# A hybrid scan, attention and FP4 kernel: the scan's input term moves from PSUM to SBUF, six pooled banks for five, two products in 128 rows, a new order of steps

## The reference, cut to what matters

```python
x = x + scan(_layernorm(x), w_in, w_x, w_dt, b_dt, A_log, Dp)
x = x + fp4_ffn(_layernorm(x), w_gate, w_up, w_down)     # F = 704
x = x + linear_attention(_layernorm(x), W_attn, ...)     # 16 heads of 16
x = x + fp4_ffn(_layernorm(x), w_gate, w_up, w_down)

# inside scan; s is the state (16), d the feature (256)
dt  = softplus(dt_low @ w_dt + b_dt) * DT_SPAN + DT_MIN
dA  = dt[:, :, None] * A
inp_term = einsum('bdn,bn,bd->bn', dA, bt, ut)
h   = exp(dA) * h + inp_term[:, None, :]
y   = einsum('bdn,bn->bd', h, ct) + Dp * ut
```

## Time and profile before

| | us |
|---|---|
| median of 3 runs | 2318.24 (2313.72 to 2318.61) |
| the profiled execution | 2323.44 |
| its span, first to last instruction | 2321.7 |
| PE busy | 2053.9 (88%) |
| DVE busy | 2015.2 (87%) |
| ACT busy | 1857.6 (80%) |
| POOL busy | 1271.2 (55%) |

### The profile page before, as it was taken

One profiled execution on the slowest core, in us unless ns is written; L12 is line 12 of the kernel. 1 busy time (PEld: TensorE's weight loads), 2 busy tenths in 40 slices (PEclk: granted clock), 3 DMA queues, 4 the chain that ended last, 5 costly groups with the idle time before them and its releaser, 6 DMA issues. The chain is left out here.

```text
span 2321.7 us, 40659 instructions
## 1 busy us (share of the span) xinstructions
PE 2053.9 (88%) x12844; PEld 1291.1 (56%) x12844; DVE 2015.2 (87%) x3843; ACT 1857.6 (80%) x3544; POOL 1271.2 (55%) x1837
## 2 busy tenths in 40 slices
PE   2558899998989989898999989899998989989997
PEld 0225556474655646465564646556464655647574
DVE  6898988979989898998989899898989889897845
ACT  4788888897978889797888979788797978867463
POOL 6224455655645565564556556465555546554754
PEclk8669999999999999999999999999999999999999
DMA  3452322323132131423213132322323232321000
GB/s 86 121 133 60 105 57 69 85 61 95 53 94 66 50 102 46 111 54 86 74 50 95 54 99 56 93 67 59 87 62 94 58 96 58 90 63 48 6 6 12
DMA packets 104450, 165.97 MB, mean 71 GB/s; under 512 B 15458, under 2 KB 34094, under 8 KB 104238
## 3 DMA queue, kind: packets, MB, share of 16 engines
q1 hardware_dynamic: 104238, 163.37, 26.2%
HBM read 146.55 MB, written 16.78 MB: 70 GB/s over the span
## 5 line engine op out<-in xcount | busy, mean ns | idle before, releaser
L1588 DVE TENSOR_TENSOR_SCAN scan_bufs<-scan_bufs,inp_bank 128x512 f32<-128x512 f32 x512 | 614.4, 1200 | 6.0 <-ACT scan_bufs L987 4.4
L1304 PE MATMUL bank<-w_gu,f_xqT 128*128 128x512 f32 x1024 | 489.1, 623 | 31.6 <-ACT f_xqT L1050 29.3
L981 ACT ACTIVATE scan_bufs<-scan_bufs,a_rows 128x512 f32<-128x512 f32 x512 | 368.9, 724 | 34.5 <-DMA scan_bufs<-dt_copy 34.2
L1319 PE MATMUL bank<-w_dn,f_hqT 128*128 128x256 f32 x1536 | 360.2, 385 | 11.2 <-ACT f_hqT L1050 9.2
L1598 DVE TENSOR_TENSOR scan_bufs<-scan_bufs,c_bank 128x512 f32<-128x512 f32 x512 | 344.0, 672 | 0.3
L1304 PEld LDWEIGHTS bank<-w_gu,f_xqT 128*128 128x128 f32 x1024 | 197.2, 199 | 255.6 <-issue 246.8
L1319 PEld LDWEIGHTS bank<-w_dn,f_hqT 128*128 128x128 f32 x1536 | 286.6, 191 | 80.1 <-issue 33.0
L898 POOL TENSOR_SCALAR_AFFINE_SELECT masked_scores<-masked_scores 128x512 f32<-128x512 f32 x256 | 172.4, 699 | 242.8 <-ACT masked_scores L1050 241.5
L876 POOL TENSOR_TENSOR f_h<-f_h,f_h_scale 128x704 f32<-128x704 f32 x128 | 185.7, 1451 | 180.5 <-DVE f_h L1468 180.5
L987 ACT ACTIVATE scan_bufs<-scan_bufs 128x1024 f32<-128x1024 f32 x256 | 271.6, 1061 | 1.0
L887 POOL TENSOR_TENSOR f_h<-f_h,f_h_lean 128x704 f32<-128x704 f32 x128 | 222.3, 1737 | 85.6 <-DVE f_h L1649 72.6
(11 more groups left out here) (198 smaller groups left out, 4393.9 us busy)
## 6 DMA issues: line engine op xcount, KB each, us to landing
scan_bufs<-dt_copy SPq DMA_DIRECT2D x512, 256.0 KB, 4.1
...
```

Source lines behind the costliest of these rows:

```text
L981: nc.scalar.activation(half, half, ACT.Exp, scale=a_rows[:, c, at:at + 1]).then_inc(root_ready, 1)
L1304: last = nc.tensor.matmul(to[:, :], f.xqT[:, k, :], w_gu[:, k, g, lo:hi], start=(k == 0), stop=(k == DH - 1))
L1319: last = nc.tensor.matmul(to[:, 0:D], f.hqT[:, k, :], w_dn[:, k, :], start=(k == 0), stop=(k == FK - 1))
L1588: nc.vector.tensor_tensor_scan(half, half, inp[:, :], 0.0, ALU.mult, ALU.add)\
```

## The change

- `inp` is an SBUF tile. Its bank joins the pool, which now has six.
- dt0 and C multiply all 128 rows of `low`. The rows that are added meet zeros in `w_dt` and in `sel_bc`. dt1 and B stay as they are.
- A new table `QUARTER` moves a step by another amount in each quarter of a batch's tiles or halves. `HEAD`, `TIMES`, `GAPS` and `SHIFT` have new numbers throughout, so each engine's order is another one; number and kind of the steps are the same.

```diff
+QUARTER = {
+    "pe": {
+        ("G", "sum"): (-0.171, 0.209, 0.263, 0.587),
...
 TIMES = {
     "dve": {
-        ("P", "inp"): 30.972, ("M", "scan"): -0.789, ("M", "read"): -0.053, ("S", "skip"): -0.882,
+        ("P", "inp"): 31.015, ("M", "scan"): -0.82, ("M", "read"): -0.104, ("S", "skip"): -0.235,
...
     at += SHIFT.get(b, {}).get(engine, {}).get((part, step), 0.0)
+    of = QUARTER.get(engine, {}).get((part, step), (0,))
+    at += of[len(of) * t // PARTS_AT[part][2]]
     return round(BEATS * b + at, 6)
...
-        b_rep = sb("b_rep", [P, T])
+        b_rep, inp = sb("b_rep", [P, T]), sb("inp", [P, T])
...
-        acc_y, c_rep, inp = bank("acc_y"), bank("c_bank"), bank("inp_bank")
-        banks = [bank(f"bank{j}") for j in range(5)]
+        acc_y, c_rep = bank("acc_y"), bank("c_bank")
+        banks = [bank(f"bank{j}") for j in range(6)]
...
-                    last = nc.tensor.matmul(to[:, :], w_dt[0:RANK, 0:P], low[0:RANK, :], start=True, stop=True)
+                    last = nc.tensor.matmul(to[:, :], w_dt[:, 0:P], low[:, :], start=True, stop=True)
...
-                nc.tensor.matmul(c_rep[:, :], sel_bc[RANK:P, 1, :], low[RANK:P, :], start=True, stop=True).then_inc(c_ready, 1)
+                nc.tensor.matmul(c_rep[:, :], sel_bc[:, 1, :], low[:, :], start=True, stop=True).then_inc(c_ready, 1)
```

More of the change, by code:

```diff
@@ L43 @@
     "sp": [
-        (38.977, "P", 0, "load"), (-70.85, "P", 0, "keep0"), (-46.269, "P", 0, "keep1"),
+        (48.732, "P", 0, "load"), (-89.381, "P", 0, "keep0"), (-44.063, "P", 0, "keep1"),
     ],
     "dve": [
[17 rows of a table removed]
[17 rows of a table added]
     ],
     "pool": [
[8 rows of a table removed]
[8 rows of a table added]
     ],
     "act": [
[13 rows of a table removed]
[13 rows of a table added]
     ],
     "pe": [
[6 rows of a table removed]
[6 rows of a table added]
     ],
@@ L102 @@
 PARTS_AT = {"P": (0, 0, 1), "M": (32, 1, 32), "Q": (33, 2, 16), "D": (32, 2, 16), "G": (32, 4, 8), "S": (48.95, 16, 2), "Y": (65.0, 1, 2), "R1": (66, 3, 4), "R2": (95.7, 7, 4)}
[L104 removed]
+GAPS = {(0, 'G'): -2.025, (1, 'P'): -98.277, (0, 'Y'): 3.289, (1, 'G'): -0.339, (0, 'R1'): 0.008, (1, 'Y'): -0.04, (0, 'R2'): -0.103, (1, 'R1'): 0.011, (1, 'R2'): -0.017, (14, 'P'): -29.235, (14, 'G'): -0.218, (15, 'P'): 62.155, (14, 'Y'): 4.957, (15, 'G'): -0.245, (14, 'R1'): 0.086, (15, 'Y'): 3.933, (14, 'R2'): -0.092, (15, 'R1'): -0.064, (15, 'R2'): 2.749, (0, 'M'): 0.01, (0, 'S'): 5.888, (1, 'M'): 0.004, (1, 'S'): -4.152, (14, 'M'): -0.008, (14, 'S'): -0.812, (15, 'S'): -3.686, (0, 'Q'): 0.02, (1, 'Q'): 0.074, (14, 'Q'): 0.04, (15, 'Q'): -0.045, (0, 'D'): -0.262, (1, 'D'): -1.37, (14, 'D'): 0.125, (15, 'D'): -0.038}
@@ new lines @@
+QUARTER = {
+    "pe": {
+        ("G", "sum"): (-0.171, 0.209, 0.263, 0.587),
+        ("Y", "turn"): (-0.128, -1.357),
+        ("R1", "turn_x"): (-0.558, -0.745, -0.179, -0.521),
+        ("R1", "up0"): (-1.275, -0.957, -0.1, -1.066),
+        ("R1", "up1"): (-1.489, -0.824, -0.606, -0.638),
+        ("R1", "turn_h"): (0.639, 0.094, -0.124, 0.081),
+        ("R1", "down"): (1.134, 0.063, -0.374, 0.216),
+        ("R1", "a_turn"): (-0.732, -1.231, -0.712, -1.257),
+        ("R1", "a_qkv"): (0.362, 0.332, 0.26, 0.513),
+        ("R1", "a_s0"): (-1.125, -0.405, -0.488, -0.105),
+        ("R1", "a_s1"): (-0.227, -0.137, -0.484, 0.734),
+        ("R1", "a_sum"): (-0.416, -0.809, 0.098, 0.656),
+        ("R1", "a_flip"): (-0.669, -0.543, -0.265, 0.638),
+        ("R1", "a_turn_y"): (-0.15, -0.095, 1.332, 0.555),
+        ("R1", "a_proj"): (-0.698, -0.022, 1.326, 1.704),
+        ("R2", "turn_x"): (-0.64, -0.724, -0.748, 0.482),
+        ("R2", "up0"): (-1.176, 0.713, -1.164, -0.236),
+        ("R2", "up1"): (-0.715, -1.09, 0.125, -0.154),
+        ("R2", "turn_h"): (-0.555, -0.163, -0.921, 0.714),
+        ("R2", "down"): (1.015, 0.358, 0.259, 1.544),
+    },
+    "dve": {
+        ("M", "scan"): (-0.038, -0.147, 0.093, -0.011),
+        ("M", "read"): (-0.022, 0.137, 0.531, -0.016),
+        ("S", "skip"): (-0.123, -0.586),
+        ("Y", "finish"): (-0.506, -1.56),
+        ("R1", "stats"): (-0.655, -1.683, -1.868, -2.895),
+        ("R1", "aggr"): (-0.439, -0.452, -1.054, -0.97),
+        ("R1", "max_x"): (-1.079, -0.867, -0.632, -0.561),
+        ("R1", "scale_x"): (-0.537, -0.127, 0.21, 0.301),
+        ("R1", "norm"): (-0.349, -0.07, 0.286, 0.282),
+        ("R1", "lean_x"): (-0.539, -0.244, -0.115, -0.02),
+        ("R1", "round_x"): (0.023, 0.382, 0.489, 0.347),
+        ("R1", "gate0"): (-0.418, -0.131, -0.37, -0.014),
+        ("R1", "gate1"): (-0.333, 0.127, 0.27, 0.381),
+        ("R1", "max_h"): (-0.083, -0.102, 0.142, -0.214),
+        ("R1", "scale_h"): (0.098, -0.061, 0.357, -0.192),
+        ("R1", "inv_h"): (0.202, 0.028, 0.415, 0.022),
+        ("R1", "lean_h"): (-0.102, -0.113, 0.006, 0.256),
+        ("R1", "round_h"): (0.069, -0.1, 0.153, 0.186),
+        ("R1", "down"): (1.533, 0.438, 0.265, 0.408),
+        ("R1", "a_stats"): (0.368, -0.369, -0.186, -0.895),
+        ("R1", "a_aggr"): (1.094, 0.222, 0.553, -0.024),
+        ("R1", "a_qkv"): (-0.244, -0.021, 0.159, 0.432),
+        ("R1", "a_sum"): (-0.333, 0.03, 0.656, 2.17),
+        ("R1", "a_den"): (-0.48, -0.064, 0.171, -0.415),
+        ("R1", "a_rden"): (-0.142, 0.054, 0.37, -0.13),
+        ("R1", "a_add"): (-27.081, 1.158, 0.764, -6.193),
+        ("R1", "a_flip"): (-0.395, -0.099, 0.193, 0.364),
+        ("R1", "a_proj"): (-0.841, 0.151, 0.618, 1.269),
+        ("R1", "stats2"): (-1.523, -0.771, -0.155, 1.251),
+        ("R1", "aggr2"): (-1.784, -0.758, -0.192, 0.972),
+        ("R2", "max_x"): (-1.226, -2.298, -2.379, -2.304),
+        ("R2", "scale_x"): (-0.202, -0.768, -1.139, -1.277),
+        ("R2", "norm"): (0.785, 0.03, -0.308, -0.202),
+        ("R2", "lean_x"): (1.035, -0.226, -0.157, 0.41),
+        ("R2", "round_x"): (-0.027, -0.679, -0.846, -0.448),
+        ("R2", "gate0"): (0.778, 0.629, -0.104, 0.745),
+        ("R2", "gate1"): (0.085, 0.284, 0.717, 0.398),
+        ("R2", "max_h"): (-0.181, 0.041, 0.314, -0.067),
+        ("R2", "scale_h"): (0.137, 0.47, 0.241, 0.09),
+        ("R2", "inv_h"): (0.023, 0.417, 0.203, 0.013),
+        ("R2", "lean_h"): (-0.285, 0.134, -0.108, 0.377),
+        ("R2", "round_h"): (-0.242, 0.396, -0.093, 0.684),
+        ("R2", "down"): (-0.259, 0.431, -0.167, 2.673),
+    },
+    "act": {
+        ("M", "decay"): (0.063, -0.507, -0.681, -0.033),
+        ("Q", "square"): (0.088, -0.28, 0.009, 0.042),
+        ("R1", "norm"): (-0.069, -0.108, -0.386, -0.004),
+        ("R1", "abs_x"): (0.002, -0.798, -0.621, -0.111),
+        ("R1", "turn_x"): (-0.448, -0.079, -0.114, 0.292),
+        ("R1", "up0"): (-2.183, -1.202, -1.078, -0.967),
+        ("R1", "copy_u0"): (-0.407, -0.1, 0.797, 0.569),
+        ("R1", "up1"): (-1.242, -1.462, -0.837, -1.265),
+        ("R1", "copy_u1"): (-0.57, -0.066, 0.791, 0.375),
+        ("R1", "abs_h"): (-0.39, 0.122, -0.219, 0.112),
+        ("R1", "turn_h"): (-0.28, 0.135, -0.539, 0.215),
+        ("R1", "a_norm"): (-0.276, 0.091, -0.026, -0.792),
+        ("R1", "a_turn"): (-0.558, -0.228, -0.275, -0.182),
+        ("R1", "a_root"): (-0.448, -0.077, -0.207, 0.271),
+        ("R1", "a_qkv"): (-0.426, -0.034, 0.08, 0.146),
+        ("R1", "a_v"): (-1.027, 0.265, -0.711, 0.527),
+        ("R1", "a_q"): (0.645, 0.336, 0.427, 0.408),
+        ("R1", "a_s0"): (0.019, 0.013, 0.374, 0.588),
+        ("R1", "a_s1"): (-0.111, -0.554, 0.072, 0.199),
+        ("R1", "a_sum"): (0.275, 0.225, 0.65, 0.659),
+        ("R1", "a_turn_y"): (-0.427, 0.109, 0.666, 1.719),
+        ("R2", "norm"): (0.227, 0.205, -3.355, -2.281),
+        ("R2", "abs_x"): (0.831, -0.031, -0.263, -0.142),
+        ("R2", "turn_x"): (0.142, -0.64, -1.21, 0.364),
+        ("R2", "up0"): (-0.918, -0.344, -1.426, -0.288),
+        ("R2", "copy_u0"): (0.352, 0.613, 0.387, 0.832),
+        ("R2", "up1"): (-0.657, -0.281, 0.044, -0.025),
+        ("R2", "copy_u1"): (-0.538, -0.939, -0.155, -0.086),
+        ("R2", "abs_h"): (0.073, 0.087, 0.075, 0.13),
+        ("R2", "turn_h"): (-0.955, 0.265, -0.288, 1.456),
+    },
+    "pool": {
+        ("R1", "stats"): (-1.995, -0.329, -0.747, -0.663),
+        ("R1", "below"): (-1.414, 0.43, -0.24, 0.072),
+        ("R1", "norm"): (-0.243, -0.377, -0.245, 0.41),
+        ("R1", "round_x"): (0.082, -0.654, -0.215, -0.093),
+        ("R1", "gate_up"): (-0.796, -0.129, -0.525, -0.713),
+        ("R1", "up1"): (0.093, 0.644, 0.711, 0.783),
+        ("R1", "round_h"): (0.134, -0.295, -0.355, 0.138),
+        ("R1", "down"): (0.868, 0.32, 1.126, 0.768),
+        ("R1", "a_below"): (1.057, 0.87, 1.082, 1.157),
+        ("R1", "a_s0"): (0.106, 0.003, 0.826, 0.481),
+        ("R1", "a_s1"): (0.382, 0.588, 1.379, 0.471),
+        ("R1", "a_proj"): (-0.654, 0.732, -0.16, 2.815),
+        ("R1", "below2"): (-1.703, -0.365, 2.468, 6.764),
+        ("R2", "norm"): (1.815, 1.386, 1.939, 1.859),
```

(28 more changed lines are left out.)

## The result

The changed kernel takes **2460.01 us** (median; 2459.21 to 2461.85), the kernel before 2318.1 us in the same comparison: a ratio of 1.0618, 95% interval 1.0599 to 1.0636. That is +142 us. The forecast was +53 us and its range ended at 2432, so the sign was right and the size much too small. The profiled execution has a span of 2458.6 us.

A forecast was written before the change was run, and what follows sets the result against it. TensorE (88%) and VectorE (87%) were both close to full. 150 us of scan waits make VectorE fullest; at 5.25% idle, after the bank's 31.1 us, that is +53 us: 2376 profiled, 2371 as median, range 2284 to 2432.

The forecast's parts named there:

- The scan contends: VectorE's scan, both operands in SBUF, and GpSimd instructions reading SBUF block each other; likeliest case, 2321 to 2412 us, chance 0.60.
- Rival A: The scan does not contend and stays at 1200 ns; only bank, order and rows count: 2284 us, chance 0.17.
- What the scans wait: VectorE's 512 scans wait for GpSimd's instructions: 150 us taken, the middle between 103 and 189 us.
- What the others of VectorE wait: Only the scans' 150 us were added to VectorE's work, 1551.6 us in the middle stretch; nothing for its other instructions.
- What GpSimd waits: 193 of GpSimd's 944 multiplications and masks start inside a scan and would wait 150 us for its end in all.
- rival C: GpSimd's FFN chain becomes the limit, a quarter to a half of its waits passed on: 2409 to 2446 us, chance 0.10.
- The price of a delay: Middle stretch: VectorE becomes fullest with 1551.6 us of work, keeps 5.25% idle, making 1637.6 us, +42.6; whole span +53.
- Rival B: The scan contends, but VectorE's idle time swallows it if no more than 2.7% stays idle: 2312 us, chance 0.13.
- The order and the bank: Sixth bank gives at most 31.1 us of TensorE's middle-stretch waits; nothing counted from the order's 24.4 us data wait.
- The signs announced: Scan's mean about 1500 ns, longer GpSimd tails, VectorE busy some 2165 us, TensorE's bank waits below 15 us.
- The lone products: TensorE's products dt0 and C, now in 128 rows, go from 1.03 to 0.89 us; 5 us taken in all.
- At the first place shown: Behind `gate1`, GpSimd's product waits 1.2 us for the scan and is ready for `f_h_max` 1.2 + 1.7 us after `gate1`.

The follow-up runs named there:

- new_sbuf_noread: Changed kernel with GpSimd's 944 large instructions replaced by fills that only write, so its output differs; 2261.19 us, ratio 0.9759 to the kernel before.
- old_sbuf: Kernel before, own order, five pooled banks, with only the scan's input term moved to SBUF; 2515.66 us, ratio 1.0853.
- pool_longer: Kernel before, input term in PSUM, plus a write-only fill of 270 columns ahead of each of GpSimd's 944 large instructions; 2393.04 us, ratio 1.033.
- dve_longer: Kernel before, input term in PSUM, plus a VectorE reduction of 256 columns ahead of each of the 512 scans; 2404.44 us, ratio 1.0374.
- old_sbuf_six: Kernel before, own order, with the scan's input term in SBUF and the freed bank as sixth in the pool; 2518.4 us, ratio 1.0874.

## Why the prediction was right in sign and wrong in size

- **The scan contends: right.** The mechanism read from the earlier trace rows holds for the scan, in both directions, and `new_sbuf_noread` shows that it needs GpSimd's reads. Rival A falls. The Trainium skill's rule ("SBUF — State Buffer", "Who interferes with whom") is borne out for the scan, down to its exception: a GpSimd instruction that only writes does not hold up a VectorE instruction with two SBUF inputs (1209 ns beside the fills, 1489 beside the reads).
- **What the scans wait: right, with some luck.** 150 us taken, 148 us measured. It was the middle between 103 and 189 us, and in the old order the same wait is 174 us (`old_sbuf`).
- **What the others of VectorE wait: left out.** VectorE's busy time rose by 177 us, not by 150. The sum had treated the waits of all other instructions as unchanged; `lean` takes 34 us more, `round` on the same tile 22 us less, the scale on x 10 us more.
- **What GpSimd waits: mis-sized by more than half, and priced at nothing.** I worked out 150 us for 944 large instructions, and used it only in rival C. It was 335 us. The large instructions took 210 us more, and the 832 small steps of the norms, which the 150 left out, 131 us: a one-column step waits as long for a scan as a large one does. That an instruction which was held up starts the next one late, inside the next scan, may have added to the 210; it is not shown.
- **The price of a delay: the step that failed.** The sum let the fullest engine keep 5.25% of idle time, and took GpSimd's idle time, 44% of the middle stretch, as room. In the changed kernel VectorE, the fullest, keeps 7.7% idle, and TensorE 12.5%. Put into the forecast's own sum, VectorE's 177 us instead of 150 make +81 us instead of +53, and with 7.75% instead of 5.25% idle they make +136; measured +142. So the idle share is the larger mistake, and `pool_longer` shows one source of it: work on GpSimd alone, busy for no more than 63%, lengthened the kernel by 75 us, where the rule had 0 to 15. The rows show where the delay is passed on. The longest waits of TensorE and of VectorE in the middle stretch are now for GpSimd:

```profile
PE bank L1443 <- POOL f_h L1006: 34.3, 29, 2.1
PE bank L1418 <- POOL f_x L1006: 29.3, 38, 2.0
```

```profile
DVE f_h_max L1602 <- POOL f_h L1017: 39.3, 44, 1.9
```

  Before, TensorE's wait for `f_x` there was 14.6 us (9 times) and the largest was for the copy `f_xqT`; VectorE's wait for GpSimd's `f_h` was 0.4 us. The VectorE part of the rule was not far out: for the 155 us of `dve_longer`, which keeps five banks, it gives +58 us with 5.25% idle and +101 with the 7.2% of before; measured +86, at 6.0% idle.
- **Rival B: wrong.** Idle time took up some of each added us (0.44 of it by `dve_longer`), but far from all. VectorE did not come near the 2.7% of idle time on which this rested; it kept 7.7%.
- **Rival C: the right mechanism, too small.** It said +38 to +75 us on top of the forecast, and its range ended at 2446. The 335 us of GpSimd cost some 70 us by the price of 0.21, up to 103 by that of 0.31.
- **The order and the bank: two errors that nearly cancel.** I counted on nothing from the order. The bank came in only through the idle share, 5.25% instead of 7.2%, which in the sum is worth 43 us. With the large reads gone, the runs show 14 us for the bank and 37 for order and products, 51 in all; with them (`old_sbuf_six`) the bank gave nothing. That the total fits is luck.
- **The signs announced.** The scan's mean and the longer tails came, VectorE's busy time is 2192 us for 2165. The waits for banks on TensorE did not fall below 15 us: one group alone, the transposes of `f_h` behind the addition that empties their bank (L1443, L1746), waits 15.3. The lone products went to 0.93 us, not 0.89, and at C that is the new neighbour's doing.
- **At the first place shown**, GpSimd's product was to wait 1.2 us behind the scan, and VectorE's `f_h_max` in its turn. One such case is in the timeline above, at 1059.38: 2.54 us for 1.69. The row above bears out the second part: `f_h_max` waited 44 times, 0.9 us each.
